# A decoder layer on one core: GpSimd's k of a group set ahead of two of the four powers of the heads' norm

## The chip, the cores and the metric

One core of one Trainium2 chip runs the whole kernel. Its engines are TensorE (PE in the profile, PEld for its weight loads), VectorE (DVE), ScalarE (ACT), GpSimd (POOL) and SyncE (SP, which here only issues DMAs). The metric is device microseconds of one execution. Each engine has its own list of instructions, written out by hand in this kernel; the engines meet only at semaphores.

## The reference

Sixteen sequences of 256 tokens and 256 features go through an attention over the heads of a single token, a cross attention and a mixture of eight low-rank adapted feed-forward experts, each with a norm in front and a residual behind. Only the first part bears on this change:

```python
xn = rms(layernorm(x), g1)
Q, K, V = (xn @ W.T for W in (Wq, Wk, Wv))      # 16 heads of 16 features
pQ, pK = elu(Q), elu(K)                         # elu(z) = max(z, 0) + exp(min(z, 0)) - 1
attn = w1 - lmb * w2                            # heads of ONE token attend to each other
attn = (1 - LAMBDA_INIT) * rms(attn, g2)        # norm of each head: 1/sqrt(mean of 16 squares + eps)
attn = rms(attn, g3) + attn                     # norm of the whole token
```

The sequences are taken in eight groups of two, 512 tokens each, which are four token tiles (0 to 3) of 128 tokens on 128 partitions.

## The kernel before, in words

A group passes through four sorts of work, and each engine's list interleaves the sorts of several groups, so that in one step of the loop (some 20 us) an engine projects one group, multiplies the heads of another and norms a third. The lists are made by `over_all` (line 132), which goes through the steps t and in each through a hand-written list of pairs (lag, function), calling the function for group t - lag; behind it stand single calls `go(group, function...)`. All of it is unrolled.

- Projection of a group: DVE takes the moments (`p_moments`) and normalises (`p_normalise`), TensorE transposes and projects. Q and K come in four blocks of 128 features by 512 tokens: `project(0)` and `(1)` are q, `project(2)` and `(3)` are k. On each block ScalarE makes the exponential (`p_exps`, lines 1229 and 1231), DVE adds the positive part (`p_elus`, line 1620), and GpSimd takes off the 1 and scales (`p_final`, line 2036). `p_final(c)` waits for `p_elus(c)` of the same group (line 2029). `p_exp`, in which the blocks stand, has two buffers, so `p_exps` of a block also waits for the `p_final` two blocks before.
- Rows of heads: SP moves q (`tiles_in(0, ...)`), k (`tiles_in(1, ...)`, line 581) and v (`values_in`, line 596) into another layout. The first k tile waits for `p_final(3)`. In SP's list the k tiles of a group stand behind its q tiles and the first four of its sixteen v transfers.
- Heads: `head_scores`, `head_masked` (DVE, line 1653), `head_values` and `head_turn` give the attention of a group in natural layout, `h_wn`.
- Norms: ScalarE squares (`head_squares`, line 1404), DVE sums per head (`head_sums`, line 1862), GpSimd makes the means (`head_mean`, line 2104) and raises them to the power -1/2, one instruction of 128x16 for each token tile (`head_rstd(0)` to `(3)`, line 2112). DVE multiplies (`head_normal`, line 1868, which waits for all four powers, then `head_gain`, line 1874); then ScalarE, GpSimd (`head_rthird`) and DVE (`head_added`, line 1880) do the norm of the whole token, and SP stores.

DVE's list in a step t is the following (line 1911), in which the number is the lag:

```python
[(4, head_masked(0, 1)), (1, p_moments), (3, but(1, p_elus(3))), (2, p_low(0)), (4, only(0, fold_low)), (2, p_low(1)),
 (6, head_normal), (6, head_gain), (5, head_sums), (2, p_elus(0)), (4, head_masked(1, 0)),
 (4, head_masked(1, 1)), (1, p_normalise), (2, p_elus(1)), (2, p_elus(2)), (3, head_masked(0, 0)), (6, head_added)]
```

TensorE's list (line 1097) has in a step `head_scores(1)`, `project(1)`, `project(2)` (which waits for `p_elus(0)`, line 795), `head_scores(0)` (which waits for the two multiplies of `head_masked(1, ...)`, line 824), `project_v(0)`, `project(3)`, and then heads, transposes and `project(0)` of the next group.

GpSimd's list is at line 2137, with two more places behind it (lines 2139 to 2148). Its step begins with the powers of token tiles 2 and 3 (lag 7), then has the two blocks of k (lag 4), the root for the first norm (`p_rstds`), and then `head_mean`, the powers of tiles 0 and 1 and the blocks of q.

Of the kernel before, what the change touches and what calls it, by code (L numbers as in the profile page):

```python
# [31 lines left out]
SU = UNITS // 2  # L32
# [48 lines left out]
def nth(u, per_unit, k, loops=0):  # L81


    return u.index * per_unit + (k + loops * UNITS * per_unit)
# [30 lines left out]
def go(n, *emits):  # L115


    for emit in emits:
        emit(Unit(0, n, n))
# [12 lines left out]
def over_all(units, stages, first, steps):  # L132


    for t in range(first, steps):
        for lag, emit in stages:
            if 0 <= t - lag < units:
                emit(Unit(0, t - lag, t - lag))


def decoder(nc, x, ctx_512, Wq, Wk, Wv, lam, g1, g2, g3, W1, W2,
            xWq, xbq, xWk, xbk, xWv, xbv, wi, bi, wo, bo, lora_A, lora_B, gate_w, gate_b, out):
    assert x.shape == (UNITS, T, D)
    with ExitStack() as ctx:
# [322 lines left out]
        def apart(eng):  # L467


            eng.sem_inc(s_passed, 1)  # L470
# [1527 lines left out]
        def _(pool):  # L1998
# [28 lines left out]
            def p_final(c):  # L2027
                def emit(u):
                    pool.wait_ge(p_elud, nth(u, 4, c + 1))
                    if c == 0 and not u.has(1):  # L2030
                        pool.wait_ge(s_foldlo, 1)
                    if c == 0 and u.has(2):
                        for k in range(2):
                            pool.wait_ge(h_qkin[u.slot][k], u.turn * 64)
                    apart(pool)
                    pool.tensor_scalar(p_qk[:, u.slot, c], p_exp[:, c % 2], -1.0, headfac[:, 0:1] if c < KD else 1.0,
                                       ALU.add, ALU.mult).then_inc(p_fin, 1)
                return emit
# [67 lines left out]
            def head_rstd(i):  # L2106

                def emit(u):
                    pool.wait_ge(h_msd, nth(u, 1, 1))
                    if i == 0 and u.has(1):  # L2110
                        pool.wait_ge(h_n1d, nth(u, 1, 0))
                    pool.tensor_tensor(h_rh[:, H * i:H * i + H], h_ms[:, H * i:H * i + H], mhalf[:, 0:H], ALU.pow).then_inc(h_rhd, 1)  # L2112
                return emit
# [6 lines left out]
            def adapters_set():  # L2120
# [13 lines left out]
            go(0, p_final(2), p_final(3))  # L2134
            go(2, p_rstds)
            go(1, p_final(0), p_final(1))
            over_all(SU, [(7, head_rstd(2)), (7, head_rstd(3)), (4, p_final(2)), (4, p_final(3)), (2, p_rstds), (6, head_mean),
                          (6, head_rstd(0)), (3, p_final(0)), (7, head_rthird), (6, head_rstd(1)), (3, p_final(1))], 5, WHOLE)
            go(3, head_rstd(2), head_rstd(3))
            go(6, p_final(2), p_final(3))  # L2140
            go(4, head_mean)
            go(7, p_final(0))
            go(4, head_rstd(0))
            go(3, head_rthird)
            go(4, head_rstd(1))
            go(7, p_final(1))
            go(4, head_rstd(2), head_rstd(3))
            go(7, p_final(2), p_final(3))
            go(0, m_with_x)
            go(5, head_mean, head_rstd(0))  # L2150
            go(1, m_with_x)
# [60 lines left out]
```

## Time and profile before

| what | us |
|---|---|
| median of 3 runs | 671.92 (667.10 to 672.93) |
| the profiled execution's own time | 671.56 |
| its span, first to last instruction | 669.8 |
| PE busy | 612.4 (91%) |
| DVE busy | 476.7 (71%) |
| ACT busy | 386.2 (58%) |
| POOL busy | 366.9 (55%) |

The span is some 55 us of weights and first projections, then the groups of the heads' stage, whose GpSimd loop ends near 165 us; to about 265 us the last groups overlap with what follows, and from 300 us a loop over the sixteen sequences runs with PE busy almost without a gap. A duration of a row is that of the instructions on their engine; the time in square brackets behind a row is how long the engine had been idle before it, and who ended that.

### The profile page before, as it was taken

The numbers are of one execution on the slowest core, as the hardware profiler recorded it, in microseconds if no ns is written. First come the engines' busy times: TensorE is split into PE (matmuls) and PEld (weight loads), VectorE is DVE, ScalarE is ACT, GpSimd is POOL, SyncE is SP. The second block draws the span as 40 slices with busy tenths as digits, with TensorE's granted clock in tenths as the row PEclk, the third lists the DMA queues.
The fourth block names the chain that finished last, engine by engine and source line by source line (L and its number), as shares of the span: only waits on it lengthen the run. The fifth ranks groups of instructions, "written<-read, shape, count | busy, mean of one in ns | idle before, by whom it ended". The sixth has DMA issues, their size and how long they took to land.

```text
span 669.8 us, 21409 instructions
## 1 busy us (share of the span) xinstructions
PE 612.4 (91%) x8338; PEld 575.4 (86%) x8338; DVE 476.7 (71%) x1138; ACT 386.2 (58%) x853; POOL 366.9 (55%) x404
## 2 busy tenths in 40 slices
PE   2887999999957878889999999999999999999997
PEld 2666787887756778789999999999999999999997
DVE  8774568787555747987787776867777777877673
ACT  3563557777754757477577484664564566455432
POOL 5221178798866685677566545455456444543333
PEclk9998899999998989999999999999999999999999
DMA  8743244454354544212201311011011101100000
GB/s 227 202 121 87 56 105 107 118 142 104 94 161 122 155 145 145 52 44 79 73 18 40 127 40 40 17 57 41 1 41 41 39 0 39 39 16 1 17 17 33
DMA packets 79719, 50.27 MB, mean 75 GB/s; under 512 B 23048, under 2 KB 79632, under 8 KB 79632
## 3 DMA queue, kind: packets, MB, share of 16 engines
q1 hardware_dynamic: 79632, 49.07, 25.9%
q8 instruction: 60, 0.98, 0.7%
q14 instruction: 27, 0.22, 0.1%
HBM read 23.88 MB, written 12.58 MB: 54 GB/s over the span
## 4 chain that ended last, share of the span: by engine, by line
PE 66%; DVE 7%; issue 6%; ACT 4%; SPq 4%; POOL 3%; DMA 2%; POOLq 0%; DVEq 0%; ACTq 0%
PE banks L717 53%; PE banks L839 4%; PE banks L770 3%; PE banks L857 3%; PE banks L875 2%; SPq L596 1%; ACT L1282 1%; DVE m_hT_lo L1664 1%; SPq L581 1%; POOL f_hT_lo L2096 1%; PE banks L782 1%; ACT m_hT_hi L1288 1%; ACT m_g L1282 1%; DMA attn_scratch<-h_wn 1%; DVE f_hs L1835 1%
## 5 line engine op out<-in xcount | busy, mean ns | idle before, releaser
L2096 POOL TENSOR_TENSOR f_hT_lo<-f_hs,f_hT_hi 128x512 fp32r<-128x512 f32 x64 | 87.0, 1360 | 112.5 <-ACT f_hT_hi L1395 112.5
L2112 POOL TENSOR_TENSOR h_rh<-h_ms,mhalf 128x16 f32<-128x16 f32 x32 | 93.8, 2939 | 2.4 <-DVE h_wn L1868 1.9
L1835 DVE SCALAR_TENSOR_TENSOR f_hs<-banks,nbic,f_h 128x256 f32<-128x256 f32 x128 | 54.6, 479 | 47.1 <-PE banks L717 47.1
L717 PE MATMUL banks<-woT_hi,f_hT_lo 128*128 128x256 f32 x256 | 74.4, 291 | 0.3 <-POOL f_hT_lo L2096 0.3
L717 PE MATMUL banks<-f_adT_hi,lbT_lo 128*128 128x256 f32 x256 | 73.0, 285 | 0.6 <-DVE f_adT_lo L1823 0.6
L717 PE MATMUL banks<-f_adT_hi,lbT_hi 128*128 128x256 f32 x256 | 71.7, 280 | 0.0
L717 PE MATMUL banks<-f_xT_hi,wiT_lo 128*128 128x256 f32 x256 | 71.7, 280 | 0.0
L717 PE MATMUL banks<-f_adT_lo,lbT_hi 128*128 128x256 f32 x256 | 71.6, 280 | 0.0
L717 PE MATMUL banks<-f_xT_lo,wiT_hi 128*128 128x256 f32 x256 | 71.5, 279 | 0.0
L717 PE MATMUL banks<-f_xT_hi,wiT_hi 128*128 128x256 f32 x256 | 71.5, 279 | 0.0
L717 PE MATMUL banks<-woT_hi,f_hT_hi 128*128 128x256 f32 x256 | 71.1, 278 | 0.0
L717 PE MATMUL banks<-woT_lo,f_hT_hi 128*128 128x256 f32 x256 | 71.1, 278 | 0.0
L1382 ACT ACTIVATE f_h<-banks,bic 128x256 f32<-128x256 f32 x128 | 51.9, 479 | 28.6 <-PE banks L717 28.4
L1395 ACT ACTIVATE f_hT_hi<-f_hs 128x512 fp32r<-128x512 f32 x64 | 40.0, 625 | 16.8 <-DVE f_hs L1835 16.8
L717 PEld LDWEIGHTS banks<-f_adT_hi,lbT_lo 128*128 128x128 f32 x256 | 48.4, 189 | 0.9 <-DVE f_adT_lo L1823 0.9
L717 PEld LDWEIGHTS banks<-woT_hi,f_hT_lo 128*128 128x128 f32 x256 | 48.2, 188 | 0.7 <-POOL f_hT_lo L2096 0.5
L717 PEld LDWEIGHTS banks<-f_xT_hi,wiT_hi 128*128 128x128 f32 x256 | 48.4, 189 | 0.0
L717 PEld LDWEIGHTS banks<-f_adT_lo,lbT_hi 128*128 128x128 f32 x256 | 48.4, 189 | 0.0
L717 PEld LDWEIGHTS banks<-f_xT_hi,wiT_lo 128*128 128x128 f32 x256 | 48.3, 189 | 0.0
L717 PEld LDWEIGHTS banks<-f_adT_hi,lbT_hi 128*128 128x128 f32 x256 | 48.2, 188 | 0.0
L717 PEld LDWEIGHTS banks<-woT_lo,f_hT_hi 128*128 128x128 f32 x256 | 48.2, 188 | 0.0
L717 PEld LDWEIGHTS banks<-f_xT_lo,wiT_hi 128*128 128x128 f32 x256 | 48.1, 188 | 0.0
(271 smaller groups left out, 1976.6 us busy)
## 6 DMA issues: line engine op xcount, KB each, us to landing
h_qk<-p_qk SPq DMA_DIRECT2D x64, 128.0 KB, 3.1
xin<-in_x_dram SPq DMA_DIRECT2D x16, 256.0 KB, 3.2
h_v<-p_v SPq DMA_DIRECT2D x128, 32.0 KB
attn_scratch<-h_wn SPq DMA_DIRECT2D x16, 256.0 KB, 2.4
m_w<-attn_scratch SPq DMA_DIRECT2D x16, 256.0 KB, 3.4
m_x<-in_x_dram SPq DMA_DIRECT2D x16, 256.0 KB, 3.1
x_scratch<-m_y SPq DMA_DIRECT2D x16, 256.0 KB, 2.1
c_x<-x_scratch SPq DMA_DIRECT2D x16, 256.0 KB, 2.8
```

The lines of the kernel that those rows point to most:

```text
L581: sp.dma_start(h_qk[32 * i:32 * i + 32:2, u.slot, H * b:H * b + H].rearrange("e h t -> e (h t)"), p_qk[:, u.slot, KD * b:KD * b + KD, i * ...
L717: ins = pe.matmul(acc, left(a), right(b), start=first and n == 0, stop=last and n == 2, skip_group_check=skip)
L770: ins = pe.transpose(dst[:, k * T + i * P:k * T + (i + 1) * P], tile[:, i, k * P:(k + 1) * P], identf[:, :])
L839: ins = pe.matmul(bank[i][HT * c:HT * c + HT, g * HT:(g + 1) * HT], by_group[:, 1, at], by_group[:, 0, at], start=True, stop=True)
L857: ins = pe.matmul(bank[4 + c][32 * i:32 * i + HD, g * HT:(g + 1) * HT], h_v[HT * c:HT * c + HT, u.slot, :, PG * i + GR * r + g], h_sm[HT * ...
L875: ins = pe.transpose(bank[TB[q]][:, n * P:(n + 1) * P], h_wT[:, u.slot, 2 * (head % (H // 2)) + head // (H // 2), :], identf[:, :])
L1282: act.activation(m_g[:, :], hidden_bank(u)[:, :], ACT.Gelu).then_inc(m_gelu, 1)
L1382: ins = act.activation(f_h1[:, j % 2, c * T:(c + 1) * T], bank[HB[j]][:, c * T:(c + 1) * T], ACT.Relu, bias=bic[:, f:f + 1])
L1395: act.activation(flat(f_hT[j][0][:, :, :]), f_hs[:, j % 2], ACT.Copy).then_inc(f_hhi, 1)
L1835: ins = dve.scalar_tensor_tensor(out=f_hs[:, j % 2, c * T:(c + 1) * T], in0=bank[HB[j]][:, c * T:(c + 1) * T], scalar=nbic[:, f:f + 1], in ...
L2096: pool.tensor_tensor(lo, f_hs[:, j % 2], hi.bitcast(F32), ALU.subtract).then_inc(f_hlo, 1)
L2112: pool.tensor_tensor(h_rh[:, H * i:H * i + H], h_ms[:, H * i:H * i + H], mhalf[:, 0:H], ALU.pow).then_inc(h_rhd, 1)
```

## The change

In each of three steps of the loop (t = 7, 8 and 9) and in two places behind it, GpSimd's list has `p_final(2)` and `p_final(3)`, the blocks of k, ahead of `head_rstd(2)` and `head_rstd(3)` instead of behind them. The steps t = 5 and 6 have no powers of these tiles, so nothing changes there. No instruction is added or taken away, and no wait.

```diff
-            over_all(SU, [(7, head_rstd(2)), (7, head_rstd(3)), (4, p_final(2)), (4, p_final(3)), (2, p_rstds), (6, head_mean),
+            over_all(SU, [(4, p_final(2)), (4, p_final(3)), (7, head_rstd(2)), (7, head_rstd(3)), (2, p_rstds), (6, head_mean),
                           (6, head_rstd(0)), (3, p_final(0)), (7, head_rthird), (6, head_rstd(1)), (3, p_final(1))], 5, WHOLE)
+            go(6, p_final(2), p_final(3))
             go(3, head_rstd(2), head_rstd(3))
-            go(6, p_final(2), p_final(3))
             go(4, head_mean)
             go(7, p_final(0))
             go(4, head_rstd(0))
             go(3, head_rthird)
             go(4, head_rstd(1))
             go(7, p_final(1))
+            go(7, p_final(2), p_final(3))
             go(4, head_rstd(2), head_rstd(3))
-            go(7, p_final(2), p_final(3))
             go(0, m_with_x)
```

## Rows read from the trace of the kernel before

**Rows 1.** Windows view, one step: length, then busy us of each engine (instructions), PEclk, DMA.

```profile
116.00:138.00 22.00, 21.96 (x586) 17.90 (x586) 18.32 (x29) 16.03 (x37) 18.23 (x14) 1.00 0.45 115
```

**Rows 2.** Chain that ended last, in order of time: start, us, what.

```profile
179.76 0.60 SPq L581
```

**Rows 3.** Timeline of POOL: start, us, engine, line, operation, out<-in, count [idle before <-releaser].

```profile
79.59 0.62 POOL L2036 TENSOR_SCALAR p_qk<-p_exp 128x512 f32<-128x512 f32 x1 [7.97 <-DVE p_exp L1620]
...
95.34 5.76 POOL L2112 TENSOR_TENSOR h_rh<-h_ms,mhalf 128x16 f32<-128x16 f32 x2
101.08 1.21 POOL L2036 TENSOR_SCALAR p_qk<-p_exp 128x512 f32<-128x512 f32 x2
...
144.25 2.17 POOL L2036 TENSOR_SCALAR p_qk<-p_exp 128x512 f32<-128x512 f32 x2
...
179.64 5.76 POOL L2112 TENSOR_TENSOR h_rh<-h_ms,mhalf 128x16 f32<-128x16 f32 x2
```

**Rows 4.** Timeline of DVE, the rows of the five places.

```profile
78.70 0.69 DVE L1620 SCALAR_TENSOR_TENSOR p_exp<-banks,p_exp 128x512 f32<-128x512 f32 x1 [1.53 <-ACT p_exp L1231]
...
100.73 0.66 DVE L1620 SCALAR_TENSOR_TENSOR p_exp<-banks,p_exp 128x512 f32<-128x512 f32 x1
...
102.50 1.22 DVE L1868 TENSOR_TENSOR h_wn<-h_wn,h_rh 128x1024 f32<-128x1024 f32 x1
103.75 1.22 DVE L1874 TENSOR_TENSOR h_wn<-h_wn,g2row 128x1024 f32<-128x1024 f32 x1
106.13 1.22 DVE L1862 TENSOR_REDUCE h_ss<-h_wT 128x64 f32<-128x1024 f32 x1 [1.15 <-ACT h_wT L1404]
...
108.31 2.35 DVE L1653 TENSOR_TENSOR h_sm<-banks,blockmask 128x1024 f32<-128x1024 f32 x2 [0.30 <-PE banks L839]
...
120.70 0.66 DVE L1620 SCALAR_TENSOR_TENSOR p_exp<-banks,p_exp 128x512 f32<-128x512 f32 x1
...
127.78 1.22 DVE L1862 TENSOR_REDUCE h_ss<-h_wT 128x64 f32<-128x1024 f32 x1 [1.60 <-ACT h_wT L1404]
...
139.70 1.41 DVE L1590 BATCH_NORM_STATS2 p_st<-xin 128x6 f32<-128x256 f32 x4 [0.58 <-DMA xin<-in_x_dram]
...
141.64 0.66 DVE L1620 SCALAR_TENSOR_TENSOR p_exp<-banks,p_exp 128x512 f32<-128x512 f32 x1
...
144.31 1.63 DVE L1868 TENSOR_TENSOR h_wn<-h_wn,h_rh 128x1024 f32<-128x1024 f32 x1 [0.82 <-POOL h_rh L2112]
...
147.41 1.21 DVE L1862 TENSOR_REDUCE h_ss<-h_wT 128x64 f32<-128x1024 f32 x1
...
160.76 0.69 DVE L1620 SCALAR_TENSOR_TENSOR p_exp<-banks,p_exp 128x512 f32<-128x512 f32 x1 [0.70 <-ACT p_exp L1231]
...
168.78 1.22 DVE L1862 TENSOR_REDUCE h_ss<-h_wT 128x64 f32<-128x1024 f32 x1 [1.45 <-ACT h_wT L1404]
...
181.06 0.69 DVE L1620 SCALAR_TENSOR_TENSOR p_exp<-banks,p_exp 128x512 f32<-128x512 f32 x1 [0.82 <-ACT p_exp L1231]
...
190.63 1.22 DVE L1862 TENSOR_REDUCE h_ss<-h_wT 128x64 f32<-128x1024 f32 x1 [2.01 <-ACT h_wT L1404]
```

**Rows 5.** Timeline of SP: v, then k; a k block is four issues.

```profile
100.33 2.63 SPq L596 DMA_DIRECT2D h_v<-p_v  x4
103.09 2.58 SPq L581 DMA_DIRECT2D h_qk<-p_qk  x4
```

**Rows 6.** Waits of SP's queue, 95 to 215 us: total us, times, longest.

```profile
SPq L470 <- POOL p_qk L2036: 5.8, 4, 2.6
```

**Rows 7.** Timeline of TensorE, its scores of the first place.

```profile
111.15 2.08 PEld L839 LDWEIGHTS banks<-h_qk 32*64 32x64 f32 x121 [0.36 <-issue]
...
114.79 0.49 PE L839 MATMUL banks<-h_qk 32*64 32x64 f32 x8 [1.38 <-issue]
```

**Rows 8.** Windows view, PE alone: length, busy us (instructions), PEclk, DMA.

```profile
198.00:200.00 2.00, 0.52 (x28) 0.91 0.21 47
200.00:202.00 2.00, 2.00 (x10) 0.50 0.28 52
```

## The prediction

> **What bounds the kernel now.** I read the page's busy rows first, then the windows of the stage that the change touches, the chain, and then the timelines of GpSimd, DVE, SP and TensorE side by side, because what decides here is an order and not a duration. In the windows the reader sees a step of the heads' stage in which TensorE is busy 21.96 of 22.00 us while DVE and GpSimd each have 18 [rows 1]: nothing in the step has much room. The chain runs through this stage and leaves it over SP's queue at 179.76 us [rows 2], so what delays the stage delays the end.
>
> Next the reader should look for the last input of each of the two things that change places. The powers of token tiles 2 and 3 have theirs long before: GpSimd runs them right after the work ahead of them, two in 5.76 us, at 95.34 and four more times, the last at 179.64 [rows 3]. The second block of k, `p_final(3)`, needs the fourth ELU block of DVE, which ends at 100.73 + 0.66 = 101.39, 121.36, 142.30, 161.45 and 181.06 + 0.69 = 181.75 in the five places [rows 4]. In the first place that is 6.05 us after GpSimd came to the pair (95.34), in the last 2.11 us after (179.64) [rows 3, 4]. In the old order these microseconds are filled with the powers; only then comes k, and it finds its input ready: both blocks in 1.21 us at 101.08 [rows 3].
>
> **The change part by part.** *k earlier.* With k first, `p_final(2)` runs at once (its input is older), and `p_final(3)` stands and waits for the fourth ELU block. How such a wait looks is in the trace before: at 79.59 GpSimd starts a k block after 7.97 us of idling for DVE, 0.20 us after that block's ELU ended (78.70 + 0.69 = 79.39) [rows 3, 4]. So k is done at about 101.39 + 0.20 + 0.62 = 102.21 in the first place, where it was done at 101.08 + 1.21 = 102.29: nothing gained. SP has k tiles to issue only after the v transfers that end at 102.96, and issues them at 103.09 [rows 5]. Its waits on GpSimd are 5.8 us in four times [rows 6], and the q tiles' waits are among them. The bounds of an earlier k are therefore 0 and -5.8 us; I take 0, as the k issue at 103.09 follows the v issue by 0.13 us, with k long there.
>
> *Powers later.* The two powers now start when `p_final(3)` ends: E + 0.20 + 0.62 + 5.76 = E + 6.6, where E is the end of the fourth ELU block. Queued behind them on GpSimd are `p_rstds`, `head_mean` and the q blocks. Waiting for them is DVE's `head_normal`, and DVE's list can't go round it: `head_gain`, `head_sums`, the next group's first ELU block and the two masking multiplies stand behind. `head_normal` and `head_gain` take 103.75 + 1.22 - 102.50 = 2.47 us [rows 4], so `head_sums` can start at E + 9.05. Before, it started at 106.13, 127.78, 147.41, 168.78 and 190.63, which is E + 4.74, 6.42, 5.11, 7.33 and 8.88 [rows 4]; in four of the five it even waited for ScalarE's squares, a reserve of 1.15 to 2.01 us that these differences already use up. What is left is a delay of 4.31, 2.63, 3.94, 1.72 and 0.17 us.
>
> *Does the delay reach the end?* Behind `head_sums` come the ELU block that `project(2)` waits for and the masks that `head_scores(0)` waits for. In the first place the masks end at 108.31 + 2.35 = 110.66 and the scores load their weights at 111.15 after a wait of 0.36 us [rows 4, 7]: TensorE was already paced by DVE there, so its list moves by the whole delay, and with it `project(3)`, the next exponentials and the next fourth ELU block. GpSimd's means start from the same `head_sums`, so q moves equally. The next place therefore begins late by the first delay and adds its own. Four places add 4.31 + 2.63 + 3.94 + 1.72 = 12.60 us. The fifth is behind the point where the chain has left GpSimd for SP (the last q block, then 179.76 [rows 2]), and its 0.17 us stays off the sum. I take 0.6 off because DVE's wait of 0.58 us for a load of x at 139.70 [rows 4] will have passed when all else is later. That gives +12.0 us.
>
> The trace before doesn't show what the new pauses do to TensorE's other gaps. In the first place the scores broke off for 1.38 us with nothing named but issue [rows 7], one of two such gaps in the five places; if a pause just ahead lets the instructions come in, both go and the sum is 12.0 - 2.8 = 9.2. If not, it is 12.0. I keep 12.0, as the gaps were there whether or not TensorE had waited shortly before.
>
> *Beside whom k runs.* At 144.25 two k blocks took 2.17 us instead of 1.21, and `head_normal` beside them 1.63 instead of 1.22 [rows 3, 4]. The new order parts them; what stands beside `head_normal` now is the short root behind the powers, as at 102.50, where DVE kept its 1.22 [rows 4]. I price this at nothing, since 2.47 is the undisturbed pair. The Trainium skill (GPSIMD Engine Reference, section Specifications) says that GpSimd's SBUF interfaces are shared with VectorE and that instructions of VectorE with two SBUF inputs contend. The rows at 144.25 agree with it. Taken fully on DVE in each of four places, at the 0.41 us that `head_normal` lost there, it would make the sum 13.6 instead of 12.0.
>
> **The sum.** The profiled execution's own time is 671.56 us (its span of 669.8 and 1.8 around it), 0.36 under the median of the runs, 671.92. 671.56 + 12.0 = 683.6.
>
> **The rivals.** *Part of it is absorbed.* The two gaps of TensorE shrink, or ScalarE and DVE win back a wait in each step. For it: DVE has some 3.7 us idle in a step [rows 1]. Against: TensorE has almost none, and four small reserves are already counted. Time 676.5 to 681, with 680.8 for both gaps gone.
>
> *TensorE's clock falls as well.* The new pauses of TensorE ahead of `project(2)` (up to the 4.31 us of the first place, less what `project(1)`, which waits for nothing new, still fills) are longer than the 1.38 us of rows 7. For it: in the tail a stretch with 0.52 busy of 2.00 us is followed by one at half the clock, 0.50, which is 1.2 instead of 2.4 GHz [rows 8]. Against: in a whole step of the stage the granted clock stays at 1.00 [rows 1], although TensorE pauses in each. The two microseconds at 0.50 cost 1.0 us of work [rows 8], and the fall is longer than they are, so I estimate 1 to 2 us for one; two or three of them make 685.6 to 689.6. The Trainium skill (TensorE: Matmul & The Clock Gate, section "What's actually happening") has the clock follow how busy TensorE has been; the falls in rows 8 agree.
>
> *The other side: k is worth more than the powers.* If the fourth ELU block ended before GpSimd comes to the pair, the powers would only move by the 1.21 us of k, less than the 1.4 us between their end (95.34 + 5.76 = 101.10) and `head_normal` (102.50) [rows 3, 4], and k would reach SP 5.76 us sooner. Its place is SP's queue, its price at most the 5.8 us that SP waits for GpSimd [rows 6], and it decides from the point at which E lies before GpSimd's arrival. In all five places E lies 2 to 6 us behind it. If the steps shifted so that it did hold, 671.56 - 0.5 to - 5.8 = 666 to 671.
>
> *It does nothing.* The order changes but `head_normal` is late anyway, as at 144.31, where DVE already waited 0.82 us [rows 4]. Then only 1.21 us moves in a place and the time is 671 to 673. Against it: in the first place `head_normal` follows at 102.50 without a wait [rows 4].
>
> **How the numbers follow.** Forecast 0.73; part absorbed 0.10; clock too 0.10; other side 0.03; nothing 0.04. A measurement of this kernel can tell about 1%, 6.7 us, from no change: the runs before lie 5.8 us apart. The forecast's own range is 680.8 (gaps gone) to 685.6 (contention, or one fall of the clock). To leave no more than 2 in 10 out I go down into the absorbed case, 676, and up to the clock's, 690. Slower by over 1% is above 678.6: the forecast, the clock and most of the absorbed case, 0.90; within 1% the rest of it, the nothing case and part of the other side, 0.08; faster 0.02.
>
> **What would show it.** In the changed profile GpSimd should idle ahead of the second k block with DVE's line 1620 as releaser, in five places and for 2 to 6 us; `head_normal` should wait for the powers in each step and start 6.6 us after the fourth ELU block; the step should grow from about 20 to 22.5 to 24 us; SP's first k tile should still follow directly behind a v transfer; and from 300 us on nothing should differ but the shift. The prediction is wrong if `head_sums` comes less than E + 9, if the delays of the places don't add up (a step that shrinks by as much as its pause), or if the tail from 180 to 300 us gives them back.

## The result, and the profile after

The change made the kernel slower: 679.05 us (median of 6 runs, 676.17 to 682.07) against 671.58 us beside it; the ratio, estimated from the runs and not the quotient of the two medians (1.0111), is 1.0129, with a 95% interval of 1.0079 to 1.0178, which is +8.7 us of 671.58. Run a second time it was 1.0152 (1.0107 to 1.0196), +10.2 us of 669.94. The forecast was +12.0 us, 683.6 us with a range of 676 to 690. The profiled execution of the changed kernel took 682.07 us (span 680.4), 10.5 us more than that of before.

The timeline of POOL in the changed kernel, in the first place, and then the row of the second k block in the four others. It answers to [rows 3]:

```profile
95.30 0.62 POOL L2036 TENSOR_SCALAR p_qk<-p_exp 128x512 f32<-128x512 f32 x1
100.99 0.62 POOL L2036 TENSOR_SCALAR p_qk<-p_exp 128x512 f32<-128x512 f32 x1 [5.07 <-DVE p_exp L1620]
101.57 5.77 POOL L2112 TENSOR_TENSOR h_rh<-h_ms,mhalf 128x16 f32<-128x16 f32 x2
...
125.48 0.62 POOL L2036 TENSOR_SCALAR p_qk<-p_exp 128x512 f32<-128x512 f32 x1 [3.80 <-DVE p_exp L1620]
...
148.27 0.62 POOL L2036 TENSOR_SCALAR p_qk<-p_exp 128x512 f32<-128x512 f32 x1 [2.69 <-DVE p_exp L1620]
...
170.43 0.62 POOL L2036 TENSOR_SCALAR p_qk<-p_exp 128x512 f32<-128x512 f32 x1 [1.68 <-DVE p_exp L1620]
...
192.58 0.62 POOL L2036 TENSOR_SCALAR p_qk<-p_exp 128x512 f32<-128x512 f32 x1 [1.68 <-DVE p_exp L1620]
```

The first k block runs at once; the second stands 1.7 to 5.1 us with the fourth ELU block of DVE as releaser, in all five places. Only then come the 5.77 us of powers, which before had filled this wait.

The timeline of DVE in the changed kernel answers to [rows 4]; the first place is given up to the masks, the others with the fourth ELU block and the sums:

```profile
100.14 0.66 DVE L1620 SCALAR_TENSOR_TENSOR p_exp<-banks,p_exp 128x512 f32<-128x512 f32 x1
...
107.37 1.22 DVE L1868 TENSOR_TENSOR h_wn<-h_wn,h_rh 128x1024 f32<-128x1024 f32 x1 [5.22 <-POOL h_rh L2112]
108.63 1.22 DVE L1874 TENSOR_TENSOR h_wn<-h_wn,g2row 128x1024 f32<-128x1024 f32 x1
109.77 1.21 DVE L1862 TENSOR_REDUCE h_ss<-h_wT 128x64 f32<-128x1024 f32 x1
110.90 0.68 DVE L1620 SCALAR_TENSOR_TENSOR p_exp<-banks,p_exp 128x512 f32<-128x512 f32 x1
111.50 2.34 DVE L1653 TENSOR_TENSOR h_sm<-banks,blockmask 128x1024 f32<-128x1024 f32 x2
...
124.59 0.69 DVE L1620 SCALAR_TENSOR_TENSOR p_exp<-banks,p_exp 128x512 f32<-128x512 f32 x1 [0.32 <-ACT p_exp L1231]
...
134.26 1.21 DVE L1862 TENSOR_REDUCE h_ss<-h_wT 128x64 f32<-128x1024 f32 x1
...
147.42 0.66 DVE L1620 SCALAR_TENSOR_TENSOR p_exp<-banks,p_exp 128x512 f32<-128x512 f32 x1
...
157.05 1.21 DVE L1862 TENSOR_REDUCE h_ss<-h_wT 128x64 f32<-128x1024 f32 x1
...
169.55 0.69 DVE L1620 SCALAR_TENSOR_TENSOR p_exp<-banks,p_exp 128x512 f32<-128x512 f32 x1 [0.81 <-ACT p_exp L1231]
...
179.48 1.22 DVE L1862 TENSOR_REDUCE h_ss<-h_wT 128x64 f32<-128x1024 f32 x1 [0.18 <-ACT h_wT L1404]
...
191.70 0.69 DVE L1620 SCALAR_TENSOR_TENSOR p_exp<-banks,p_exp 128x512 f32<-128x512 f32 x1 [0.82 <-ACT p_exp L1231]
```

Read each place as a distance from the end E of its fourth ELU block (100.80, 125.28, 148.08, 170.24, and 192.39 in the fifth place). `head_normal` starts at E + 6.57 or 6.58 in each; the sums start at E + 8.97, 8.98, 8.97 and 9.24, where they started at E + 4.74, 6.42, 5.11 and 7.33 [rows 4]. In the first three places nothing stands in brackets behind the sums: they follow DVE's own list, in the first and second place instead of ScalarE's squares. From E to the next E it was 19.97, 20.94, 19.15 and 20.30 us, and is now 24.48, 22.80, 22.16 and 22.15.

The chain that ended last in the changed kernel, some of its pieces in the first place (start, us, what):

```profile
100.22 0.59 DVE p_exp L1620
...
101.57 5.78 POOL h_rh L2112 x2
...
107.37 1.24 DVE h_wn L1868
...
109.77 1.00 DVE h_ss L1862
...
110.90 0.69 DVE p_exp L1620
...
111.64 2.78 PE banks L717 x6
```

In the first place this is the prediction's path piece by piece: ELU block, powers, `head_normal`, sums, the next ELU block, and `project(2)` of TensorE that waits for it. In the second place the same chain takes GpSimd's branch behind the sums: the means (135.70), a q block (138.92), the root of the whole token (140.05) and `head_added` (143.22) lead to the next fourth block. From the third place it runs over the masks, TensorE's heads and ScalarE's squares (178.39) to the sums of the fourth, so that the powers of the fourth place are not on it. SP's timeline, to set beside [rows 5]:

```profile
98.34 2.63 SPq L596 DMA_DIRECT2D h_v<-p_v  x4
101.70 3.31 SPq L581 DMA_DIRECT2D h_qk<-p_qk  x4
```

The k tiles leave 0.73 us after the v issues, not 0.13, because SP has to wait for k here: its v issues end at E + 0.17, before at E + 1.57 [rows 5]. Counted from E, k goes out at E + 0.90 instead of E + 1.70, so 0.80 us sooner. It wins nothing: the scores that read k start 0.51 us behind the end of the masks here (111.50 + 2.34 = 113.84, then 114.35) and 0.49 us behind it before (110.66, then 111.15 [rows 7]). In the four other places k follows the v issues by 0.12 or 0.13 us.

### The profile page after: what moved, and what is told of

It reads as the page before. It is cut to its first block, busy times and chain, and to the rows that moved or that the text cites. A ratio compares the mean times of both kernels' runs of the same rounds, so it can differ in the third digit from the quotient of the medians.

```text
span 680.4 us, 21409 instructions
## 1 busy us (share of the span) xinstructions
PE 616.2 (91%) x8338; PEld 576.4 (85%) x8338; DVE 475.2 (70%) x1138; ACT 386.0 (57%) x853; POOL 371.5 (55%) x404
## 4 chain that ended last, share of the span: by engine, by line
PE 56%; DVE 10%; issue 8%; POOL 6%; SPq 5%; ACT 5%; DMA 2%; POOLq 0%; DVEq 0%; ACTq 0%
PE banks L717 48%; PE banks L770 3%; POOL h_rh L2112 3%; SPq L596 3%; PE banks L839 2%; ACT L1282 1%; SPq L581 1%; DVE m_hT_lo L1664 1%; PE banks L857 1%; POOL f_hT_lo L2096 1%; DVE h_ss L1862 1%; DMA xin<-in_x_dram 1%; ACT m_hT_hi L1288 1%; ACT h_t L1420 1%; ACT m_g L1282 1%
## 5 line engine op out<-in xcount | busy, mean ns | idle before, releaser
L717 PE MATMUL banks<-p_xT_hi,wqkvT_lo 128*128 128x512 f32 x96 | 44.3, 461 | 7.2 <-DVE p_exp L1620 3.8
```

The source lines that it names most:

```text
L717: ins = pe.matmul(acc, left(a), right(b), start=first and n == 0, stop=last and n == 2, skip_group_check=skip)
```

## The experiments

Each stood beside the kernel before on the same chip; the intervals are 95%.

**1. The change again.** No edit.

> The changed kernel once more, beside the kernel before and the three others of this set. Theory (GpSimd waits for the fourth ELU block with the powers behind it): 8 to 11 us above the kernel before, and head_sums 9.0 us after the fourth ELU block in the first four places. A rival, that the 8.7 us are an accident of TensorE's clock in some executions, has it within 4 us of the kernel before.

Measured: 679.95 us (675.99 to 682.03) against 669.94, 1.0152 (1.0107 to 1.0196), and the sums at E + 8.98, 8.98, 8.98 and 8.97. The slowdown is no accident of single executions. What differs most between the two profiles of this same kernel is the clock; first a stretch of the run here (length, busy us of PE, granted clock, DMA, GB/s):

```profile
164.00:166.00 2.00, 0.48 (x14) 0.62 0.18 40
166.00:170.00 4.00, 4.00 (x16) 0.50 0.02 4
```

and the same stretch of the profile above, with both rows at 1.00:

```profile
164.00:166.00 2.00, 1.30 (x12) 1.00 0.10 22
166.00:170.00 4.00, 3.55 (x124) 1.00 0.11 25
```

The step from the third place to the fourth took 24.80 us here and 22.16 there. Of these 2.6 us some 0.3 are a longer break of the scores just before (1.52 against 1.18 us), so the fall of the clock is worth some 2.3 us in the step where it comes, and it doesn't come each time. At the end it doesn't show: this profiled execution took 681.06 us, the other 682.07.

**2. Only the first k block ahead.**

```diff
-[(7, head_rstd(2)), (7, head_rstd(3)), (4, p_final(2)), (4, p_final(3)),
+[(4, p_final(2)), (7, head_rstd(2)), (7, head_rstd(3)), (4, p_final(3)),
```

The two places behind the loop are edited likewise.

> Only the first k block goes ahead of the two powers; the second, whose input comes late, stays behind them. Theory: no wait arises, since the first block's input is ready, and the powers move by its 0.62 us, which head_normal's reserve takes up but in the third place, where it already waited: 0 to +1 us against the kernel before. The rival that it is the order as such (k beside the DVE multiplies of that moment, the buffer freed early) has half of the change's cost, some +4 us.

Measured: 670.81 us, 1.0021 (0.9993 to 1.0050), +1.4 us with an interval that holds zero. The timeline of POOL in the first place:

```profile
93.21 0.62 POOL L2036 TENSOR_SCALAR p_qk<-p_exp 128x512 f32<-128x512 f32 x1
93.79 5.76 POOL L2112 TENSOR_TENSOR h_rh<-h_ms,mhalf 128x16 f32<-128x16 f32 x2
99.53 0.62 POOL L2036 TENSOR_SCALAR p_qk<-p_exp 128x512 f32<-128x512 f32 x1
```

No row has a wait in brackets. Half of k ahead of the powers is at most a small part of the cost; it is the block whose input is late that matters.

**3. One power ahead of k and one behind.**

```diff
-[(7, head_rstd(2)), (7, head_rstd(3)), (4, p_final(2)), (4, p_final(3)),
+[(7, head_rstd(2)), (4, p_final(2)), (4, p_final(3)), (7, head_rstd(3)),
```

The two places behind the loop are edited likewise.

> One power ahead of both k blocks and one behind. Theory: head_normal starts 0.20 + 0.62 + 2.88 = 3.7 us after the fourth ELU block and head_sums 6.2 us after it, against 4.74, 6.42, 5.11 and 7.33 before, so 1.4 + 0 + 1.1 + 0 = +2.5 us. The rival that any wait of GpSimd ahead of a power costs what the change costs has +8 to +11 us.

Measured: 672.71 us, 1.0045 (1.0013 to 1.0076), +3.0 us. GpSimd waits as in the changed kernel, but half as much stands behind the wait. DVE's timeline in the first place:

```profile
100.05 0.66 DVE L1620 SCALAR_TENSOR_TENSOR p_exp<-banks,p_exp 128x512 f32<-128x512 f32 x1
...
104.42 1.23 DVE L1868 TENSOR_TENSOR h_wn<-h_wn,h_rh 128x1024 f32<-128x1024 f32 x1 [2.52 <-POOL h_rh L2112]
...
106.82 1.21 DVE L1862 TENSOR_REDUCE h_ss<-h_wT 128x64 f32<-128x1024 f32 x1
```

`head_normal` starts 104.42 - 100.71 = 3.71 us after the block, as worked out (3.7), and the sums at E + 6.11. In the second and fourth place the sums wait for ScalarE's squares (1.24 and 2.53 us), so there it is no longer the powers that set when they start. The cost follows what is queued behind the wait.

**4. The moved powers made cheap.**

```diff
-    pool.tensor_tensor(h_rh[...], h_ms[...], mhalf[:, 0:H], ALU.pow)
+    pool.tensor_tensor(h_rh[...], h_ms[...], mhalf[:, 0:H], ALU.mult if i >= 2 and u.index <= 4 else ALU.pow)
```

> The order of the change, but the ten powers of token tiles 2 and 3 that it moves are multiplications of the same size (the root of those two tiles is left out). Theory: GpSimd waits for the fourth ELU block as in the changed kernel, but behind it stand some 0.6 us instead of 5.76, so head_normal comes about 1.5 us after the block and DVE waits as little as before: -1 to +1 us against the kernel before. The rival that the cost lies in k's place itself, or in TensorE's gaps, keeps +8 us.

Measured: 668.77 us, 1.0001 (0.9972 to 1.0029). POOL's timeline in the first place:

```profile
98.80 0.62 POOL L2036 TENSOR_SCALAR p_qk<-p_exp 128x512 f32<-128x512 f32 x1 [4.76 <-DVE p_exp L1620]
99.38 0.40 POOL L2112 TENSOR_TENSOR h_rh<-h_ms,mhalf 128x16 f32<-128x16 f32 x2
```

The wait is there, 4.76 us long, and the time is that of before, to within 1.9 us: 0.40 us behind the wait is early enough for DVE. So the wait of GpSimd by itself is not the price; the powers behind it are. One thing stays open in this run alone: the short powers also take work off GpSimd, and the old order with short powers was not run, so that a cost of the wait and a gain from the shorter work could cancel. Experiment 9, in which the powers keep their length, speaks against it.

**5 to 7. The places taken apart.** The order of the change in the first and third place alone, in the fifth alone, and in the second and fourth alone; `k_blocks_of` and `k_blocks_but` stand for both k blocks of the named groups and of all others:

```diff
 # 5: only for the k of groups 3 and 5 (7: group 4, and the first place behind the loop)
+[(4, k_blocks_of((3, 5))), (7, head_rstd(2)), (7, head_rstd(3)), (4, k_blocks_but((3, 5))), (2, p_rstds), 
 # 6: the second place behind the loop
+go(7, p_final(2), p_final(3))
 go(4, head_rstd(2), head_rstd(3))
-go(7, p_final(2), p_final(3))
```

> The change in the first and third place alone. Theory: each place costs by itself what head_sums comes later there, 8.98 - 4.74 = 4.2 and 8.97 - 5.11 = 3.9 us, less some 1 us that the next step gives back: +6 to +8 us against the kernel before. The rival that the cost is shared by all five (TensorE loses its rhythm once) has +10 for any two of them, or hardly anything.

> The change in the fifth place alone, behind the last q block of GpSimd. Theory: the delay of head_normal there is taken up by the wait for ScalarE's squares and by what SP's queue sets, so 0 to +0.5 us. The rival that every wait of GpSimd is paid has +2 us; that the last k block comes some 5 us sooner and is worth it, -1 us or less.

> The change in the second and fourth place alone, where head_sums had waited for ScalarE's squares before. Theory: 8.98 - 6.42 = 2.6 and 9.0 - 7.33 = 1.7 us, less up to 1 us given back: +3 to +4.5 us. The rival that each place pays the whole wait for the fourth block plus its powers, with no reserve, has +8 us, as much as the first and third place.

Measured against 668.88 us: first and third 675.88, 1.0090 (1.0058 to 1.0121), +6.0 us; second and fourth 672.46, 1.0039 (1.0009 to 1.0069), +2.6 us, a little under what was said; the fifth 671.86, 1.0018 (0.9990 to 1.0046), +1.2 us, which doesn't tell 0.5 from 2. The three add up to 1.47%, and the change as a whole had 1.29% and 1.52%: the places are paid one by one, and dearer where the sums had stood nearer behind the fourth block (E + 4.74 and 5.11 in the first and third place, 6.42 and 7.33 in the second and fourth). In the fifth place alone, `head_normal` waited 6.57 us and k was not wanted sooner; SP's timeline there:

```profile
187.46 2.63 SPq L596 DMA_DIRECT2D h_v<-p_v  x4
190.20 3.13 SPq L581 DMA_DIRECT2D h_qk<-p_qk  x4
```

The k tiles follow the v issues by 0.11 us: here SP comes to k when its own list lets it.

**8. `head_normal` behind the masks in DVE's list.** GpSimd as in the change. DVE's list is edited in the steps of the loop, ScalarE's also in the first place behind it.

```diff
 # DVE
-(6, head_normal), (6, head_gain), (5, head_sums), (2, p_elus(0)), (4, head_masked(1, 0)), (4, head_masked(1, 1)),
+(5, head_sums), (2, p_elus(0)), (4, head_masked(1, 0)), (4, head_masked(1, 1)), (6, head_normal), (6, head_gain),
 # ScalarE
-(7, head_squares3), (3, but(1, p_exps(1))), (3, but(1, p_exps(2))),
+(3, but(1, p_exps(1))), (3, but(1, p_exps(2))), (7, head_squares3),
```

> The changed kernel's GpSimd list; in DVE's list head_normal and head_gain stand behind the sums, the first ELU block and the two masks of the next scores, and ScalarE's squares of the whole token behind its second and third exponentials. Theory (DVE's queue behind head_normal carries the delay): the masks end some 10.5 us after the fourth ELU block or sooner instead of 13.2, and the cost falls to +1 to +5 us; GpSimd's own queue (its means now behind the powers) keeps the rest. The rival that GpSimd's queue alone carries it keeps +8 to +11 us.

Measured: 693.56 us, 1.0344 (1.0299 to 1.0389), +23.0 us. The expectation failed. Its first half held: the masks ended at 109.21, E + 9.47, before the 10.5 that was expected. But POOL's timeline shows two new waits:

```profile
110.49 3.87 POOL L2112 TENSOR_TENSOR h_rh<-h_ms,mhalf 128x16 f32<-128x16 f32 x1 [2.50 <-DVE h_wn L1868]
...
118.18 0.20 POOL L2014 TENSOR_SCALAR h_m<-h_s 128x4 f32<-128x4 f32 x1 [3.14 <-ACT h_t L1412]
```

The first power of the next group overwrites `h_rh` and must wait until `head_normal` has read it; and the root of the whole token waits for squares that ScalarE now does later. Both hold up the last q block on GpSimd, and that the exponentials. This experiment changed more than one thing, so it tells nothing about the carrier; the next one does.

**9. `head_normal` without the wait.** GpSimd's list as in the change, powers late and all.

```diff
-dve.wait_ge(h_rhd, nth(u, ST, ST))
+dve.wait_ge(h_rhd, nth(u, ST, 2 if u.index <= 4 else ST))   # and h_rh[:, 0:2 * H] for both halves
```

> The changed kernel with GpSimd's list as it is, powers late and all, but for the first five groups head_normal waits for the powers of token tiles 0 and 1 alone and uses them for tiles 2 and 3 too (the norm of tiles 2 and 3 is left out there). Theory: what carries the delay is DVE's list behind head_normal, so head_sums comes no later than before and most of the cost goes; GpSimd's means start behind powers and root at about 7.9 us after the fourth ELU block instead of 6.2, 7.9, 6.3 and 8.8, which leaves +1 to +3 us. The rival that GpSimd's own list carries the delay keeps +8 to +11 us.

Measured: 670.96 us against 670.85, 1.0010 (0.9983 to 1.0036). The timelines of POOL, and of DVE, in the first place:

```profile
101.60 5.76 POOL L2118 TENSOR_TENSOR h_rh<-h_ms,mhalf 128x16 f32<-128x16 f32 x2
...
108.81 0.25 POOL L2110 TENSOR_SCALAR h_ms<-h_ss 128x64 f32<-128x64 f32 x1
```

```profile
100.16 0.66 DVE L1620 SCALAR_TENSOR_TENSOR p_exp<-banks,p_exp 128x512 f32<-128x512 f32 x1
101.93 1.21 DVE L1871 TENSOR_TENSOR h_wn<-h_wn,h_rh 128x1024 f32<-128x1024 f32 x1
...
105.69 1.22 DVE L1862 TENSOR_REDUCE h_ss<-h_wT 128x64 f32<-128x1024 f32 x1 [1.28 <-ACT h_wT L1404]
```

The powers are as late as in the change (101.60), GpSimd's means start at E + 8.0, and the time is that of before: +0.7 us, with an interval from -1.1 to +2.4. What carries the cost is thus the one instruction of DVE that waits for the powers, with the list behind it. GpSimd's own lateness, for which +1 to +3 us was expected, doesn't show clearly in the time, though the lower part of that range isn't excluded. In the stage itself it does leave a trace: in the second and fourth place the sums came at E + 8.53 and 9.33, with ScalarE's squares as releaser, and from the first to the fifth fourth block this profile took 85.13 us, that of before 80.36.

## Why the prediction was right

- *k gains nothing.* Right in what it is worth: in the first place k was done at 101.61, E + 0.81 (predicted E + 0.82), and the scores waited for the masks, not for k. The sign that SP's first k tile should follow directly behind a v transfer held in four places; in the first SP waited 0.73 us for k.
- *`head_normal` at E + 6.6, sums at E + 9.05.* Measured E + 6.57 and, in four places, E + 8.97 to 9.24. The delays were 4.23, 2.56, 3.86 and 1.91, together 12.56 us, where 4.31, 2.63, 3.94 and 1.72, together 12.60, had been worked out from rows of before. Experiments 3, 4 and 9 show that this term is the cause: halve it, shrink it or take DVE's wait away, and the cost goes with it.
- *What the steps give back.* From E to E the four steps grew by 4.51, 1.86, 3.01 and 1.85, together 11.23: between sums and the next fourth block 1.33 us came back, where 0.6 was predicted. This is a term a little too small. That the list moves by the whole delay was also a little too much: in the first place the masks ended at E + 13.04 instead of E + 9.27, 3.77 us later and not 4.23.
- *The reserves.* All these differences stand on one profile of the kernel before, and prediction and measurement subtract the same numbers from it; that 12.56 and 12.60 come out so close therefore tests only E + 9.05. The profile of experiment 6 has the order of before up to its fifth place, so it is a second one. Its DVE timeline, the fourth ELU block of the first place, that block and the sums of the second, and the block of the fifth:

```profile
99.67 0.66 DVE L1620 SCALAR_TENSOR_TENSOR p_exp<-banks,p_exp 128x512 f32<-128x512 f32 x1
...
119.40 0.66 DVE L1620 SCALAR_TENSOR_TENSOR p_exp<-banks,p_exp 128x512 f32<-128x512 f32 x1
...
127.93 1.22 DVE L1862 TENSOR_REDUCE h_ss<-h_wT 128x64 f32<-128x1024 f32 x1 [2.39 <-ACT h_wT L1404]
...
182.51 0.69 DVE L1620 SCALAR_TENSOR_TENSOR p_exp<-banks,p_exp 128x512 f32<-128x512 f32 x1 [0.83 <-ACT p_exp L1231]
```

  There the sums stood at E + 4.70, 7.87, 5.92 and 7.25, which makes the delays 4.27, 1.11, 3.05 and 1.99, together 10.42. From the first to the fifth fourth block it took 82.87 us, where the profile of before took 80.36 and that of the changed kernel 91.59: a growth of 8.72 and not 11.23. So the reserves differ by some 2 us in sum from one execution to the next, and the forecast of +12.0 read them from an execution in which they were small; this alone is about as much as it lies above +10.2.
- *The delay reaches the end.* How much of it does is not settled. GpSimd's last q block and the first root of the cross attention, before and then in the changed kernel:

```profile
178.59 1.08 POOL L2036 TENSOR_SCALAR p_qk<-p_exp,headfac 128x512 f32<-128x512 f32 x1
...
222.32 0.19 POOL L2014 TENSOR_SCALAR c_ve<-c_mv 128x2 f32<-128x2 f32 x1 [10.35 <-DVE c_mv L1578]
```

```profile
189.24 1.07 POOL L2036 TENSOR_SCALAR p_qk<-p_exp,headfac 128x512 f32<-128x512 f32 x1
...
231.35 0.19 POOL L2014 TENSOR_SCALAR c_ve<-c_mv 128x2 f32<-128x2 f32 x1 [9.75 <-DVE c_mv L1578]
```

  The q block was 10.65 us late, the root only 9.03 us. In experiment 1's profile these are 13.64 and 8.72 us (192.23 and 231.04). So 1.6 to 4.9 us were missing behind the heads. Whether the change gives them back isn't settled: that stretch lasted 43.7 us in the profile of before and 42.1 in that of the changed kernel, but also 41.7 to 43.8 us in the profiles of experiments 2 to 7 and 9, which have little of the delay or part of it; only experiment 1's 38.8 and experiment 8's 40.3 lie below. The measured +8.7 and +10.2 lie below the 12.0 by 3.3 and 1.8.
- *TensorE's gaps.* I kept them in the sum, and they stayed: in the step of the first place the scores of the changed kernel again broke off, for 1.67 us (1.38 in [rows 7]), and in that of the third for 1.18 us (1.38 before).
- *The clock.* The rival came true in part, inside the forecast's range. PE alone, in the first place of the changed kernel's profile (length, busy, clock, DMA, GB/s):

```profile
108.00:112.00 4.00, 1.77 (x7) 0.98 0.22 49
112.00:114.00 2.00, 2.00 (x6) 0.50 0.22 49
...
120.00:122.00 2.00, 2.00 (x6) 0.50 0.23 56
```

  Ahead of the first fall to 0.50, the lower level of 1.2 GHz, TensorE was busy for 1.77 of 4.00 us. Yet this step grew by 4.51 us, hardly more than its delay of 4.23: most of these two falls was hidden, and what shows is a wait of DVE for ScalarE of 0.32 us ahead of the next fourth block (124.59 above). In experiment 1 a fall in the third step did cost some 2.3 us there. The two rivals without a slowdown fell: the fourth ELU block came behind GpSimd's arrival in every place, and the powers moved by the whole wait.
- *Beside whom k runs.* `head_normal` and `head_gain` took 1.22 us each, as priced; the loss of 0.41 us a place that would have made 13.6 was not seen there. It was GpSimd that stretched: the scaling of `p_rstds` (128x4) took 1.23 us beside them in three places (107.42, 131.91 and 154.70), and 0.19 to 0.20 in experiment 9, where DVE had no such multiply going.

## What to carry to other kernels

Before two instructions of one engine change places, compare when the last input of each is ready with when the engine gets there: here the instruction that was ready belonged ahead of the one that wasn't. The price is not the wait itself (4.76 us of it, with little behind, cost nothing that the runs could tell) but what stands behind it, seen from the next in-order list that needs it; that list's reserve is to be taken off place by place, and read from more than one profile where there is one. To find who carries a delay, take away one wait with data that are already there, as in experiment 9; moving instructions about, as in experiment 8, can bring in waits for a buffer that cost more than the thing looked for.

## What the runs showed of the hardware that was not expected

GpSimd's power of 128x16 takes 2.88 us an instruction (two in 5.76), its multiplication of the same shape 0.20 us (two in 0.40). And the clock of one and the same kernel is not the same in each execution: the stretch from 164 to 170 us ran at 1.00 in one and with four microseconds at 0.50 in the other, although `head_normal` stood at E + 6.57 and E + 6.58 in the place before. Whether the two ran on the same chip isn't known.
